# The last group of a two-layer graph network: logits tile by tile, probabilities turned round on TensorE, output passes regrouped

## The reference

```python
h = jnp.einsum('bnd,ade->bane', feat_in, W)
th = jnp.tanh(h)
attn = attn_src + jnp.swapaxes(attn_dst, 2, 3)      # th @ w_src, th @ w_dst, per head
attn = jnp.where(attn >= 0, attn, LEAKY_ALPHA * attn)
attn = jnp.where(mask, jnp.float32(-999.0), attn)
attn = jax.nn.softmax(attn, axis=-1)
feat_out = jnp.einsum('banm,bame->bane', attn, h) + b
feat_out = jax.nn.elu(feat_out)
gate = jax.nn.sigmoid(feat_in @ H_w.T + H_b)
return gate * feat_out + (1.0 - gate) * feat_in
```

## Time and profile before

| | |
|---|---|
| median of 3 runs | 2523.59 us (2522.96 to 2524.67) |
| the profiled execution, its time | 2525.22 us |
| its span (first to last instruction) | 2523.4 us |
| mean granted TensorE clock | 0.991 |
| busy: TensorE, VectorE, ScalarE, GpSimd | 98%, 80%, 36%, 32% of the span |

### The profile page before, as it was taken

How to read it: one execution, slowest core, us unless ns; L and a number is a source line. 1 busy time by engine, 2 the same in 40 slices (tenths; PEclk the granted TensorE clock), 3 DMA queues, 4 the chain that set the end, 5 groups by cost and what they waited for, 6 DMA issues and landing times.

```text
span 2523.4 us, 54226 instructions
## 1 busy us (share of the span) xinstructions
PE 2462.4 (98%) x22560; PEld 1754.9 (70%) x22592; DVE 2006.3 (80%) x2769; ACT 911.9 (36%) x1118; POOL 802.2 (32%) x564
## 2 busy tenths in 40 slices
PE   7999999999999999999999999999999999999994
PEld 5676677776677776777776777766777766777763
DVE  7778878778778778777788778788787788787778
ACT  5434333234333233333343333333333343332332
POOL 0123332333332333332333322333323333323333
PEclk9999999999999999999999999999999999999997
DMA  8244343343343443343443343433443433433432
GB/s 299 35 102 77 78 95 81 75 94 72 78 100 76 80 86 76 81 99 75 82 81 76 87 93 70 93 77 76 91 87 76 90 74 78 94 82 75 82 60 54
DMA packets 552303, 216.98 MB, mean 86 GB/s; under 512 B 517840, under 2 KB 527056, under 8 KB 552272
## 3 DMA queue, kind: packets, MB, share of 16 engines
q1 hardware_dynamic: 552272, 216.53, 39.8%
HBM read 67.02 MB, written 25.17 MB: 37 GB/s over the span
## 4 chain that ended last, share of the span: by engine, by line
PE 94%; DVE 4%; ACT 1%; DMA 1%; issue 0%; POOL 0%; SPq 0%; DVEq 0%; POOLq 0%; ACTq 0%
PE pair_prj L583 57%; PE pair_prj L597 30%; PE pair_att L613 3%; PE pair_att L688 2%; PE pair_att L701 1%; PE pair_att L738 1%; DVE w_lo L883 0%; DMA arena<-in_L_gnn_Wq 0%; PE pair_prj L623 0%; DVE w_top L843 0%; DVE w_hi L972 0%; SPq L484 0%; DMA arena<-arena 0%; DVE p_place L1162 0%; DVE arena L993 0%
## 5 line engine op out<-in xcount | busy, mean ns | idle before, releaser
L583 PE MATMUL pair_prj<-w_hi,arena 128*128 128x512 f16 (+1 forms) x6144 | 1445.8, 326 | 2.9 <-DVE arena L1101 2.5
L583 PE MATMUL pair_prj<-w_lo,arena 128*128 128x512 f16 (+1 forms) x3072 | 1002.0, 326 | 0.0
L583 PEld LDWEIGHTS pair_prj<-w_hi,arena 128*128 128x128 f16 x6144 | 601.6, 98 | 405.0 <-issue 3.2
L597 PE MATMUL pair_prj<-arena,w_hi 128*128 128x256 f16 x4608 | 762.5, 273 | 3.5 <-DVE w_lo L890 3.3
L597 PE MATMUL pair_prj<-arena,w_lo 128*128 128x256 f16 x2304 | 629.3, 273 | 0.0
L597 PEld LDWEIGHTS pair_prj<-arena,w_hi 128*128 128x128 f16 x4608 | 447.6, 98 | 55.6 <-issue 3.4
L583 PEld LDWEIGHTS pair_prj<-w_lo,arena 128*128 128x128 f16 x3072 | 300.9, 98 | 194.9 <-issue 0.8
L1662 POOL TENSOR_TENSOR rstd<-var_eps,minus_half 128x2 f32<-128x2 f32 x63 | 62.9, 998 | 668.3 <-DVE var_eps L908 660.9
L597 PEld LDWEIGHTS pair_prj<-arena,w_lo 128*128 128x128 f16 x2304 | 226.0, 98 | 26.6
L1679 POOL TENSOR_TENSOR arena<-arena,b_row 128x768 f32<-128x768 f32 x60 | 108.3, 1805 | 331.3 <-DVE arena L965 331.3
L1409 ACT ACTIVATE h_hi<-arena,shift,rstd 128x768 f16<-128x768 f32 x124 | 120.7, 1020 | 209.2 <-DVE shift L913 209.2
(11 more groups left out here) (181 smaller groups left out, 2841.9 us busy)
## 6 DMA issues: line engine op xcount, KB each, us to landing
arena<-in_x SPq DMA_DIRECT2D x64, 768.0 KB, 4.3
out<-arena SPq DMA_DIRECT2D x64, 384.0 KB, 2.3
arena<-arena SPq DMA_TRANSPOSE x380, 3.4
arena<-in_L_gnn_Wq SPq DMA_DIRECT2D x2, 1152.0 KB, 8.4
arena<-in_L_gnn_Wk SPq DMA_DIRECT2D x2, 1152.0 KB, 11.7
w_hi<-in_L_gnn_Wv SPq DMA_DIRECT2D x2, 1152.0 KB, 13.4
w_lo<-in_L_gnn_Wf SPq DMA_DIRECT2D x2, 1152.0 KB, 14.4
arena<-in_L_gnn_W SPq DMA_DIRECT2D x2, 1152.0 KB, 13.7
```

Of the source, the lines that this page charges most:

```text
L583: mm = nc.tensor.matmul(pair[:, lo:hi], lhs(a, k), weight(m, k, b)[:, lo:hi], start=(k == 0 and n == 0), stop=(k == KT - 1 and n == 2))
L597: mm = nc.tensor.matmul(pair[:, c * 256:(c + 1) * 256], weight(m, k, a)[:, o:o + P], (ht0_hi, ht0_lo)[b][:, k, :], start=(k == 0 and n == ...
```

## The change

It concerns steps 32 and 33 only; the loop's instructions are the same.

- `end_transpose` writes to `pair_prj` in place of `pair_att`, and loses its wait for the logits; TensorE's waits for `end_lo` ahead of the two `attend` go. The second tile's transposes stand inside `project_h(0)`, behind its wide half.
- Split, target terms, operands and logits are made for each tile by itself (`end_split`, `end_target_terms`, `end_operands`, `end_spread`, `end_logit_left`, `end_logits`), in `pair_att`. The logits of a tile stand inside its gate projection, behind the narrow half.
- The probabilities of group 31 are not split and transposed by DMA. TensorE turns them in f32 by 24 matmuls of 64x64 a tile with the identity (`end_turn`); ScalarE and VectorE split them out of PSUM (`end_probabilities_high`, `_low`), and `end_attend` multiplies graph by graph, 72 matmuls of 64x64 a tile.
- VectorE's and ScalarE's passes for group 30 stand at other places; the bias of group 31 is added by VectorE (`output_biased`), not by GpSimd; `final` does both tiles' first three passes ahead of the rest.

The diff, cut to its core and moved left; left out are names handed on, small helpers taken apart (`end_leak`, `end_mask`, `h_tanh`, `h_high`) and the same change of `pair_att` in `end_high` and `end_low`:

```diff
+end_p = [[v.rearrange("p a n -> p (a n)")[:, 0:C].rearrange("p (a n) -> p a n", a=H1) for v in pt]
+     for pt in (pt1[0], end_pt1)]
...
     if tail:
...
-        first_probabilities(j, j)
...
     if final:
-        second_probabilities()
...
+    for lo, hi in pieces:
...
-        if lo and between is not None:
+        if between is not None and (lo, hi) == pieces[0]:
             between()
...
     def end_transpose(t):
         pe.wait_ge(end_full, t + 1)
-        pe.wait_ge(z_ready, 2 * p + t + 1)
         for k in range(KT):
-            mm = nc.tensor.transpose(pair_att[t][:, k * P:(k + 1) * P], rows[:, t, k * P:(k + 1) * P],
+            mm = nc.tensor.transpose(pair_prj[t][:, k * P:(k + 1) * P], rows[:, t, k * P:(k + 1) * P],
                                      ident[:])
         mm.then_inc(end_turned, 1)
...
+    def end_operands(t):
+        pe.wait_ge(dst_terms_ready, j + t + 1)
+        pe.wait_ge(o_norm, 2 * p + t + 1)
+        nc.tensor.matmul(pair_att[t][:, 512:512 + N], dst_terms[:, t, :], node_eye[:], start=True, stop=True)\
+            .then_inc(rhs_psum, 1)
+        nc.tensor.matmul(pair_att[t][0:PARTS1, 0:P], parts[:, t, 0, :], ident_bf[:], start=True,
+                         stop=True).then_inc(lhs_psum, 1)
+    def end_logits(t):
+        pe.wait_ge(logit_lhs_ready, j + t + 1)
+        pe.wait_ge(logit_rhs_ready, 2 * j + t + 1)
+        for lo, hi in ((0, 512), (512, C)):
+            mm = nc.tensor.matmul(pair_att[t][:, lo:hi], logit_lhs[:, t, :], logit_rhs[t][:, lo:hi],
+                                  start=True, stop=True)
+        mm.then_inc(z_psum, 1)
+    def end_turn(t):
+        pe.wait_ge(exp1_ready, 2 * j + t + 1)
+        for a in range(H1):
+            for g in range(2):
+                r = slice(g * N, (g + 1) * N)
+                mm = nc.tensor.matmul(pair_att[t][r, a * N:(a + 1) * N], p1[r, t, a, :], ident[r, r],
+                                      start=True, stop=True)
+        mm.then_inc(end_turned, 1)
+    def end_attend(t):
+        pe.wait_ge(h_ready, 2 * p + t + 1)
+        pe.wait_ge(end_lo, T + t + 1)
+        hi, lo = end_p[t]
+        for a in range(H1):
+            c = slice(a * E1, (a + 1) * E1)
+            for n, (pt, hv) in enumerate(((hi, h1v_hi), (hi, h1v_lo), (lo, h1v_hi))):
+                for g in range(2):
+                    r = slice(g * N, (g + 1) * N)
+                    mm = nc.tensor.matmul(pair_att[t][r, c], pt[r, a, :], hv[r, t, c], start=(n == 0),
+                                          stop=(n == 2))
+        mm.then_inc(o_psum, 1)
...
     if tail:
         end_transpose(0)
-        pe.wait_ge(end_lo, 1)
         attend(0)
-        end_transpose(1)
-        project_h(0)
-        pe.wait_ge(end_lo, 2)
+        project_h(0, between=lambda: end_transpose(1))
         attend(1)
         project_h(1)
-        project_gate(0)
-        logit_operands()
-        logits()
-        project_gate(1)
+        end_operands(0)
+        project_gate(0, between=lambda: end_logits(0))
+        end_operands(1)
+        project_gate(1, between=lambda: end_logits(1))
+        end_turn(0)
+        end_turn(1)
+        return
+    if final:
+        end_attend(0)
+        end_attend(1)
         return
...
+def output_biased(t, p):
+    dve.wait_ge(o_norm, 2 * p + t + 1)
+    o = heads1(scratch(t, p)[0])
+    nc.vector.tensor_tensor(o, o, b1_row[:].unsqueeze(1).broadcast_to([P, H1, E1]), ALU.add)\
+        .then_inc(o_biased, 1)
...
+    def end_split(t):
+        whole, left = src_dst[:, t], rest[:, t]
+        part = parts[:, t].rearrange("p s (k a) -> p s k a", k=3)
...
+        nc.vector.tensor_copy(part[:, :, 0, :], whole).then_inc(part1_ready, 1)
...
+        dve.wait_ge(part2_ready, j + t + 1)
+        nc.vector.tensor_tensor(part[:, :, 2, :], left, part[:, :, 1, :], ALU.subtract)\
+            .then_inc(parts_ready, 1)
...
+    def end_spread(t):
+        dve.wait_ge(rhs_psum, j + t + 1)
+        nc.vector.tensor_tensor(logit_rhs[t].rearrange("p (a n) -> p a n", a=H1),
+                                pair_att[t][:, 512:512 + N].unsqueeze(1).broadcast_to([P, H1, N]),
+                                of_head[:].unsqueeze(2).broadcast_to([P, H1, N]), ALU.mult)\
+            .then_inc(logit_rhs_ready, 1)
...
+    def end_probabilities_low(t):
+        dve.wait_ge(end_hi, T + t + 1)
+        hi, lo = end_p[t]
+        nc.vector.scalar_tensor_tensor(lo, heads1(pair_att[t][:, 0:C]), P_TOP, hi, ALU.mult, ALU.subtract)\
+            .then_inc(end_lo, 1)
...
     if tail:
...
         end_offset(1)
         p1_low(1, p)
         sum_and_invert(0, p)
-        end_low(1)
         output_first(0, p)
         sum_and_invert(1, p)
         output_min(0, p)
-        output_last(0, p)
+        end_low(1)
+        output_elu(0, p)
         h_low(0)
         output_first(1, p)
+        output_gated(0, p)
         h_source(0)
         h_target(0)
+        end_split(0)
+        end_spread(0)
         output_min(1, p)
         h_low(1)
+        end_leak(0)
         h_source(1)
         h_target(1)
-        split_source_and_target()
-        gate_argument(0)
-        spread_over_heads(0)
-        spread_over_heads(1)
-        output_elu(1, p)
-        dve.wait_ge(not_adj_made, j + 1)
-        leak_and_mask(0)
+        end_split(1)
+        end_mask(0)
+        end_spread(1)
         shift1(0)
-        leak_and_mask(1)
-        p1_low(0, j)
+        end_leak(1)
+        end_mask(1)
         shift1(1)
         sum_and_invert(0, j)
+        end_probabilities_low(0)
+        gate_argument(0)
+        end_probabilities_low(1)
+        sum_and_invert(1, j)
+        output_elu(1, p)
         output_gated(1, p)
-        p1_low(1, j)
         gate_argument(1)
-        sum_and_invert(1, j)
         return
     if final:
-        output_first(0, p)
-        output_min(0, p)
+        for t in range(T):
+            output_first(t, p)
+            output_biased(t, p)
+            output_min(t, p)
         output_elu(0, p)
-        output_first(1, p)
         output_gated(0, p)
-        output_min(1, p)
         output_last(1, p)
         return
...
+    def end_logit_left(t):
+        act.wait_ge(lhs_psum, j + t + 1)
+        nc.scalar.activation(logit_lhs[0:PARTS1, t, :], pair_att[t][0:PARTS1, 0:P], ACT.Copy)\
+            .then_inc(logit_lhs_ready, 1)
+    def end_probabilities_high(t):
+        act.wait_ge(end_turned, T + t + 1)
+        nc.scalar.activation(end_p[t][0], pair_att[t][:, 0:C].rearrange("p (a n) -> p a n", a=H1), ACT.Copy,
+                             scale=P_TOP).then_inc(end_hi, 1)
...
         end_high(0)
         p1_high(1, p)
         end_normalise(1)
-        end_high(1)
         h_from_kept(0, p)
         h_from_kept(1, p)
         output_exp(0, p)
-        h_parts(0)
-        h_parts(1)
+        end_high(1)
+        h_tanh(0)
+        h_high(0)
+        h_tanh(1)
+        end_logit_left(0)
+        h_high(1)
+        logits_out(0)
         output_exp(1, p)
-        gate_tanh(0)
-        logit_left()
-        logits_out(0)
+        end_logit_left(1)
         logits_out(1)
         h_from_kept(0, j)
+        exponentials1(0, j)
         h_from_kept(1, j)
-        exponentials1(0, j)
-        p1_high(0, j)
         exponentials1(1, j)
-        p1_high(1, j)
+        end_probabilities_high(0)
+        end_probabilities_high(1)
+        gate_tanh(0)
         gate_tanh(1)
         return
     if final:
...
             in_graph[:].unsqueeze(1).unsqueeze(3).broadcast_to(shape), ALU.mult)\
             .then_inc(dst_terms_ready, 1)
...
+    def end_target_terms(t):
+        pool.wait_ge(parts_ready, j + t + 1)
+        shape = [P, 2, PARTS1]
+        nc.gpsimd.tensor_tensor(
+            dst_terms[:, t, PARTS1:3 * PARTS1].rearrange("p (g q) -> p g q", g=2),
+            parts[:, t, 1, :].unsqueeze(1).broadcast_to(shape), in_graph[:].unsqueeze(2).broadcast_to(shape),
+            ALU.mult).then_inc(dst_terms_ready, 1)
     if tail:
         end_power(1)
         add_bias(0)
+        keep_scales()
         add_h(0, p)
+        add_h(1, p)
         products(0)
         add_bias(1)
+        end_target_terms(0)
         products(1)
-        target_terms()
-        add_h(1, p)
-        keep_scales()
+        end_target_terms(1)
         add_h(0, j)
         add_h(1, j)
         return
     if final:
-        add_bias(0)
-        add_bias(1)
         return
```

More of the change, by code:

```diff
@@ L576, in weight, with project_rows @@
                 return (w_hi, w_lo)[part][:, m, k, :]
-            def project_rows(m, lhs, t, pair, done, between=None):
-                for lo, hi in ((0, 512), (512, C)) if between is None else ((512, C), (0, 512)):
+            WIDE_FIRST, NARROW_FIRST = ((0, 512), (512, C)), ((512, C), (0, 512))
+            def project_rows(m, lhs, t, pair, done, between=None, pieces=WIDE_FIRST):
+                for lo, hi in pieces:
                     for k in range(KT):
@@ L647, in end_transpose, with project_h @@
                     pe.wait_ge(end_full, t + 1)
[L648 removed]
```

(4 more changed lines are left out.)

29 lines of the change are left out of this document (24 added, 5 removed).

## The result

Over 22 runs each, the kernel before has a median of 2524.34 us (2522.79 to 2525.18) and the changed one 2520.40 us (2519.02 to 2521.95): 0.9985 of before (95% interval 0.9979 to 0.9991), 3.9 us less, with 2.3 to 5.3 within the interval. The forecast was 2.3 us less, off another median of the kernel before; both lie under the 5.0 us that were called "no change".

A forecast was written before the change was run, and what follows sets the result against it. VectorE's work, with its holds by GpSimd, was taken to bound the end. Work +2.3, held -3.4 and idle -1.2 sum to -2.3 us, giving 2521.2 from a median of 2523.59; range 2518.8 to 2523.8.

The forecast's parts named there:

- ledger: Stretch from 2454.05 booked as VectorE work 45.0 to 47.3, held 10.5 to 7.1, idle 11.0 to 9.8: -2.3 us.
- Step 1: TensorE's first waits: attend(0) starts at 2453.6 without the low part, attend(1) at 2462.0; project_h(1) ends 2469.6, against 2471.3.
- Step 2: VectorE and GpSimd alternate from 2463.6; tile 0's parts ready at 2476.2, the split by tile costing about 0.5 net.
- Step 3: Logits by tile: TensorE idle 2469.6 to 2476.5, half clock until about 2481; logits copied by 2482.2 and 2489.7.
- Step 4: Softmax of tile 1: subtraction held until 2494.2 by GpSimd's two additions (3.58), exponential ends 2496.0.
- Step 5: Turn on TensorE, 1.62 a tile; attention done by 2502.5, VectorE comes at 2505.7; TensorE's 8.79 returns almost nothing.
- Step 6: Last passes: 14 VectorE instructions with nothing between them, 12.6 us in place of 15.82, end 2518.3; gain 3.2.
- Rival A: Turns twice as dear, or TensorE at half clock for the second: it ends 1.6 later, median 2522.9; chance 0.20.
- Rival B: TensorE at full clock on restart at 2476.5, or one held pass less: median 2519.4; chance 0.17.
- Rival C: The turn becomes the bound: slower than before from about 3.9 us a turn, at 6.5 median 2529.1; chance 0.06.
- Rival D: Change does nothing, VectorE's work bounds all; with one more hold (1.8) and 0.5 of splits, median 2523.6; chance 0.09.

The follow-up runs named there:

- the best version: Changed kernel with both tiles' gates moved ahead of operands, group 31's minimum on ScalarE, GpSimd's kept-input adds after the second subtraction: 2518.17 us, 0.9975 of before.
- both gates early: Changed kernel with tile 0's gate and the wide half of tile 1's gate ahead of their operands; one execution, stretch 62.59 us.

## Why the prediction was right

It named the mechanism: VectorE bounds the end, TensorE's long wait is not the prize, and the last passes bring the gain. How near the number came is in part luck. The median of 2520.40 lies 0.8 from the forecast 2521.2, but the kernel before was at 2524.34 in these runs and not at 2523.59; the difference is 3.9 where 2.3 was forecast. In the stretch the forecast is 1.1 too long. Point by point, in us after the first low part:

| | before | forecast | after |
|---|---|---|---|
| parts of tile 0 | 28.3 (both tiles) | 22.2 | 21.4 |
| copies of logits end, tile 0 and 1 | 32.4 / 33.2 | 28.2 / 35.7 | 26.9 / 34.6 |
| exponential of tile 1 ends | 44.2 | 42.0 | 40.9 |
| first normalisations of group 31 | 50.8 / 57.0 | 51.7 / 54.1 | 50.5 / 52.9 |
| end | 66.6 | 64.2 | 63.2 |

The column "forecast" is its clock times less 2454.05; its length of 64.2 is the sum of its ledger. The ledger's split of before (work 45.0, held 10.5, idle 11.0) does not come out of the rows: by length they give 49.6, 8.7 and 8.3, with the same sum. So only its differences are of use, and of these the one for waits was too small. The forecast's range is also narrower than its own rule, since B to D with 0.8 on either side is 2518.6 to 2524.4 and not 2518.8 to 2523.8; the measured time lies in both.

Step 1: right in order, wrong in its times, and without effect. TensorE was at half clock here too, as the window over the wide half of tile 0's `project_h` shows. A row of before had it already: the 36 matmuls behind the 3.27 us of idle took 1.85, their like 1.21.

```profile
2455.00:2458.40 3.40, 3.40 (x9) 1.21 (x8) 3.30 (x6) 2.66 (x3) 0.30 (x1) 0.50 0.98 120
```

The second attention starts at 9.3 and not 8.0, and `project_h(1)` ends at 16.3 and not 15.6. TensorE only waits for tile 0's parts the shorter for it: 5.47 us and not 6.9.

Step 2: right in kind, 0.8 too long by the time tile 0's parts are there. ELU's first pass starts 0.3 earlier than booked, and from there to the last split the alternation of VectorE and GpSimd took 12.1 us (2462.98 to 2475.11), 0.5 less than booked.

Step 3: right in kind, wrong in one size. TensorE does wait for tile 0's parts (5.47 us idle) and does come back at half clock. But "I take half clock until about 2481" was too long: the granted clock is 0.50 to 2478.8 and 1.00 from 2479.0, 3.4 us after the restart. The 18 narrow matmuls take 3.50, not 3.9, and the logits 0.3, not 0.6; VectorE waits 2.18, not 2.7. This, some 0.4, with the 0.8 of step 2 is what the forecast lacks: 1.0 to 1.2 us from the first logits on, carried to the end.

Step 4: right. L1250 takes 2.25 us with GpSimd's two adds (3.59, at 2489.37) beside it; taking that hold away was part of the best version.

Step 5: the turn at 1.61 against 1.62 taken from another shape, attention at 1.32; a turn at half clock took 2.83 in "both gates early", where the bound was 3.2. The Trainium skill (TensorE: Matmul & The Clock Gate, Part 2) gives about 62 ns for each matmul where the decoding is done in microcode, which would be an estimated 4.5 us for an attention. The trace does not agree, 72 in 1.32 us are 18 ns each, so the row was right; whether the rule's condition was met here no run shows. That the 8.79 us return almost nothing is shown from both sides: the turn alone 0.6, the new order with the DMA left in place 3.3. But it holds only where something else makes the second attention early, or where the passes behind it wait for other things. With the final passes new and step 32 old, the same turn is worth 3.6 (66.62 to 63.04).

Step 6: 12.6 forecast, 12.68 measured (2504.24 to 2516.92). It is 3.1 less than the 15.82 of before, and so nearly the whole gain: steps 1 to 5, booked at 0.9 of loss, gained 0.3. The forecast gave step 6 its 3.2 as a plain term of a sum, and that was too plain. By themselves the new final passes are worth 0.0; they need the second attention to be early, by the turn or by the new order. The forecast had no place for this, since it summed steps, and it was right only because the change does all of them. One reading in the working is wrong without effect: the two last passes of before end 5.3 us apart, not 3.8 "as now"; from VectorE's last pass to the end of the span there are 2.7 us before and 2.8 after.

Rival A falls for its cause: the turns were neither dearer nor at half clock, but doubled they cost +1.3 against the 1.6 it gave. Rival B falls for its cause: TensorE came back at a granted clock of 0.50, and the held time fell by no more than booked (2.9 in this ledger, 3.4 in the forecast's). Yet its length, 62.4, lies nearer to the measured 63.2 than the forecast's 64.2. Rival C's place was right, but a turn took 1.61 us and not the 3.9 from which the kernel would be slower. Rival D falls: the interval of the ratio ends at 0.9991. What stays open: the 0.3 that the profiles differ by ahead of the stretch, of which no run says more than that such shifts come and go, and why the medians of two runs fell further than their stretches.

## What to carry to other kernels

At the end of a program, an engine's long wait is worth only what the engine that ends last waits for because of it; here 8.79 us of TensorE's wait were worth 0.6 with the old final passes, and 3.6 with the new ones. Where two waits stand beside each other, test edits singly and together: 0.6 and 0.0 became 3.6. Read "busy" of VectorE for what it holds: 8.7 us of it in this stretch were passes standing for GpSimd. An order that puts GpSimd's adds beside reductions and passes that read PSUM gets some of it back with no work saved (about 1.1 here, in the last run), but only where no other wait takes its place: the new order of step 32 saved 1.5 of holds and gained nothing.

## What the runs showed of the hardware

- In a run of 216 matmuls a tile, 64x64 in f16 at 18 ns each, TensorE stood after 101 and then every 128 records with nothing to wait for, for 0.20, 1.70 and 0.31 us. Transfers of kind "instruction" in the same stretch suggest that its instructions ran out; that is not shown. 72 in a row showed no gap.
- A matmul with f32 operands of 64x64 leaves two records: 24 are 48 records in 1.61 us at full clock, 2.83 at half.
- The granted clock fell to 0.50 while TensorE was idle for 5.47 us and came back 3.4 us after the restart; moved elsewhere, an idle stretch of 5.70 us brought half clock to 2488.4, 5.7 us after its restart. In the run with the attention three times it fell behind 1.70 us without a matmul. Where the idle time lies decides which matmuls pay.
- A pass of 12 elements a partition is held by GpSimd as well: 0.76 in place of 0.23 us.
